# The f16 low part of the middle plane is computed by GpSimd in place of VectorE, for all images but the last

## The chip, the cores and the metric

One core of one Trainium2 chip runs the whole program. The metric is the device time of one execution, in microseconds (us). Engine names are those of the profile: PE is TensorE, PEld its weight loads, DVE is VectorE, ACT is ScalarE, POOL is GpSimd, SP is SyncE, which only issues DMAs here.

## What is computed

Two residual convolution blocks on x of shape 16 x 128 x 32 x 32 (f32), 128 channels in and out, 3x3 kernels:

```python
pooled  = mean(gn(x), axis=(2, 3))
routing = sigmoid(pooled @ w_route.T + b_route)               # 4 experts per image
y       = conv3x3(gn(x), w_experts)                           # mixed over experts by routing
x       = x + silu(batch_norm(y))
x       = x + conv3x3(gn(x), sign(W))
```

`gn` is a group norm with 32 groups of 4 channels, without affine parameters. The second `gn(x)`, times 256, is the middle plane of this text.

## The kernel before, in words

Channels lie on the 128 partitions, the 1024 pixels of an image along the free dimension. All 16 images stay in SBUF in `X`. The loop over t from 1 to 15 works on several images at once, in each of the engines' own programs; what keeps them together are semaphores, and each engine runs its instructions strictly in the order in which they are written.

**First convolution of image t.** ACT and DVE mix the four experts' weights into `U` (DVE `mix`, L781, three instructions of 128x1152 for each image), DVE makes from them the kernels of a Winograd-like transform by rows (`even_rows`, L790 and L791; `kernel_rows`, L801 and L804) and from the normalised image `xn` the transformed rows (`transform_sums`, L813 and L816; `transform`, L824 to L834). PE multiplies at six points, `minus_points` into `pb`, `plus_points` into `pa`, `end_points` into `pe_`, all L402. DVE turns the products back into rows of `y` (`inverse_sums` L841 and L842, which read `pa` in PSUM; `inverse_inner` L847 to L859, SBUF only; `inverse_outer` L867, which reads `pe_` in PSUM). ACT applies the Silu (L608), a DMA from the POOL queue adds `y` to the image in `X` (`residual`, L319; for images 0, 14 and 15 DVE does it, L873 and L881), and ACT takes the variance of the result (`var_mid`, L544), squares the deviations (L551), and PE adds them up over groups (`group_vars`, L376 and L377). DVE scales (`variance`, L745), POOL raises to the power -0.5 (`power`, L315, a tiny instruction of one or two elements per partition), DVE makes the bias (`biases`, L751).

**Second convolution of image t-1.** ACT writes the middle plane twice: `hi` in f16 (L623) and `hn` in f32 (L630). DVE writes `lo = hn - hi` in f16 (`low_part`, L892, 128x1024). PE multiplies the f16 weights `ws`, the signs, first by `hi`, then by `lo` (`sign_half`, L437, 18 matmuls each over two halves, all into `pc`). ACT copies the sum out (`evacuate`, L637), and a DMA from the POOL queue adds it to the output in HBM (`add_output`, L324). `hn` has one buffer: ACT's next `hn` waits for `lo`. `hi` and `lo` have two.

**Order in an image's period on DVE** (t from 2): `mix` x3, `even_rows`, `variance`, half of `kernel_rows`, `biases`, the other half, `inverse_sums`, `inverse_inner`, `inverse_outer`, `low_part(t-1)`, `transform_sums(t+2)`, `transform(t+2)`. **On POOL:** `power(t+2)`, `add_output(t-2)`, `residual(t)`. **On PE:** `minus_points(t)`, `group_vars(t+2)`, `plus_points(t)`, `end_points(t)`, logits, `hi` products of image t-1, `lo` products of image t-1 with `group_means(t+3)` between their halves. At t=1 `low_part(0)` stands between the second and the third `mix`. At t=15 DVE's `low_part(14)` stands ahead of `residual_last`, the bn statistics of image 15 (L731) and the last group norm; the last image's `lo` is made after that.

Of the kernel before, what the change touches and what calls it, by code (L numbers as in the profile page):

```python
# [10 lines left out]
ALU = mybir.AluOpType  # L11
ACT = mybir.ActivationFunctionType

B, C, H, W = 16, 128, 32, 32
# [36 lines left out]
def build(nc, x, w_experts, w_sign, params, out):  # L51
# [6 lines left out]
    with ExitStack() as ctx:  # L58
        def sb(name, shape, dt=F32):
            return ctx.enter_context(nc.sbuf_tensor(name, shape, dt))  # L60
# [4 lines left out]
        def sem(name):  # L65
            return ctx.enter_context(nc.semaphore(name))
# [15 lines left out]
        hn = sb("hn", [C, HW])  # L82
        hi = [sb(f"hi{p}", [C, H, W], F16) for p in range(2)]
        lo = [sb(f"lo{p}", [C, H, W], F16) for p in range(2)]
# [91 lines left out]
        hi_ready = sem("hi_ready")  # L176
        hn_ready = sem("hn_ready")
        lo_ready = sem("lo_ready")
        conv_ready = sem("conv_ready")
# [9 lines left out]
        def img(i):  # L189
            return X[:, i * HW:(i + 1) * HW]  # L190

        def flat(ap):
            return ap.rearrange("p a b -> p (a b)")

        def flat3(ap):
            return ap.rearrange("p t k w -> p (t k w)")
# [19 lines left out]
        def cols(c):  # L216
            return (IN if c < LAG else MID), (2 if c < B else 1)
# [31 lines left out]
        def silus(i):  # L249

            return i + 1 + (i == B - 1)
# [22 lines left out]
        @block.sync  # L274
        def _(sp):
            def load(i):
                sp.dma_start(img(i), x_v[i, :, :]).then_inc(x_loaded[i], 16)

            def load_row(slot, row):
                sp.dma_start(we[:, :, slot, :], we_v[:, row, :, :]).then_inc(we_loaded[slot], 16)  # L280

            sp.dma_start(img(0)[:, 0:BANK], x_halves[0, 0, :, :]).then_inc(x_half_loaded, 16)
            sp.dma_start(img(0)[:, BANK:HW], x_halves[0, 1, :, :]).then_inc(x_loaded[0], 16)
            sp.dma_start(prm[:], params).then_inc(prm_loaded, 16)
            load(1)
            load_row(G1, 1)
            load_row(G0, 0)
            load_row(G2, 2)
            load(2)
            load(3)  # L290
            sp.dma_start(ws_raw[:], ws_v).then_inc(ws_loaded, 16)
            for i in range(4, B):
                sp.wait_ge(x_loaded[i - 3], 16)
                load(i)
            for i in range(B - LATE):
                wait_h(sp, i)
                sp.dma_start(out_v[i, :, :], img(i)).then_inc(h_stored[i], 16)
            done = 0
            for i in range(B - LATE, B):
                for first, last in out_parts(i):  # L300
                    done += 1
                    sp.wait_ge(out_ready, done)
                    sp.dma_start(out_v[i, :, first:last], img(i)[:, first:last]).then_inc(stored, 16)
            sp.wait_ge(stored, 16 * done)
            for p in range(2):
                sp.wait_ge(out_added[p], 16 * (B - LATE) // 2)

        @block.gpsimd
        def _(pool):
            g = nc.gpsimd  # L310

            def power(c):
                a, b = cols(c)
                pool.wait_ge(ve_ready, c + 1)
                g.tensor_tensor(rstd[:, c, a:b], ve[:, c, a:b], nhalf[:, a:b], ALU.pow).then_inc(rstd_ready, 1)  # L315

            def residual(i):
                pool.wait_ge(silu_ready, silus(i))
                g.dma_start(img(i), flat3(y[i % 2][:]), accum_op=ALU.add).then_inc(added[i % 2], 16)  # L319

            def add_output(i):
                pool.wait_ge(h_stored[i], 16)
                pool.wait_ge(evacuated, i + 1)
                g.dma_start(out_v[i, :, :], ev[i % 2][:], accum_op=ALU.add).then_inc(out_added[i % 2], 16)  # L324

            g.memset(nhalf[:], -0.5).then_inc(zeroed, 1)
            g.memset(ones[:], 1.0).then_inc(zeroed, 1)
            g.iota(gdist[:], [[GSIZE, C // GSIZE], [0, GSIZE]], base=0, channel_multiplier=-1) \
             .then_inc(gdist_ready, 1)
            for p in range(2):  # L330
                g.memset(xn[p][:, 0:PH:PH - 1, :], 0.0).then_inc(zeroed, 1)
            pool.wait_ge(zeroed, 1)
            pool.wait_ge(bn_ve_ready, 1)
            g.tensor_tensor(bn_rs[:], bn_ve[:], nhalf[:, 0:1], ALU.pow).then_inc(bn_rs_ready, 1)
            for c in range(LAG):
                power(c)
            for t in range(ND):
                if t not in DVE_RESIDUAL:
                    residual(t)
            for t in range(1, B + 1):  # L340
                power(t + LAG - 1)
                if 0 <= t - 2 < B - LATE:
                    add_output(t - 2)
                if ND <= t < B and t not in DVE_RESIDUAL:
                    residual(t)

# [349 lines left out]
        def _(dve):  # L696
# [45 lines left out]
            def variance(c):  # L742
                a, b = cols(c)
                dve.wait_ge(gvar_ready, c + 1)
                v.tensor_scalar(ve[:, c, a:b], gvar(c, a, b), 1.0 / ACT_SCALE ** 2, GN_EPS / ACT_SCALE ** 2,  # L745
                                ALU.mult, ALU.add).then_inc(ve_ready, 1)
# [11 lines left out]
            def pool_routes(c):  # L758
                if c < B:
                    dve.wait_ge(zr_ready, c + 1)  # L760
                    v.scalar_tensor_tensor(out=pooled[:, c, :], in0=wroute[:], scalar=zr[:, c:c + 1], in1=bshare[:],
                                           op0=ALU.mult, op1=ALU.add).then_inc(pooled_ready, 1)
# [74 lines left out]
            def inverse_sums(t):  # L837
                r = rank(t)
                dve.wait_ge(minus_ready, r + 1)
                dve.wait_ge(m_ready, 3 * r + 2)  # L840
                v.tensor_tensor(flat3(sums[:]), flat3(pa[:]), minus[:], ALU.add).then_inc(sums_ready, 1)  # L841
                v.tensor_tensor(flat3(diffs[:]), flat3(pa[:]), minus[:], ALU.subtract).then_inc(sums_ready, 1)  # L842
# [41 lines left out]
                    half_stats(i, half)  # L884
                aggregate(i, CHAINS - 1, MID, nm_mid_ready, var_mid_ready)

            def low_part(i):
                dve.wait_ge(hn_ready, i + 1)
                dve.wait_ge(hi_ready, i + 1 + (i == B - 1))
                if i >= 2:  # L890
                    dve.wait_ge(conv_ready, 2 * (i - 1))
                v.tensor_tensor(flat(lo[i % 2][:]), hn[:], flat(hi[i % 2][:]), ALU.subtract).then_inc(lo_ready, 1)  # L892

            def output_part(i, n):
# [43 lines left out]
            for t in range(1, B):  # L938

                c = t + LAG - 1  # L940
                if t == 1:
                    variance(c)
                    inverse_sums(t)
                    biases(c)
                    pool_routes(c)
                    inverse_inner(t)
                    inverse_outer(t)
                    mix(t + 1, 2)
                    low_part(t - 1)
                    mix(t + 1, 3)  # L950
                    even_rows(t + 1)
                    kernel_rows(t + 1, -1)
                    kernel_rows(t + 1, 1)
                else:
                    mix(t + 1, 1)
                    mix(t + 1, 2)
                    mix(t + 1, 3)
                    even_rows(t + 1)
                    variance(c)
                    kernel_rows(t + 1, -1)  # L960
                    biases(c)
                    pool_routes(c)
                    kernel_rows(t + 1, 1)
                    inverse_sums(t)
                    inverse_inner(t)
                    inverse_outer(t)
                    low_part(t - 1)
                transform_sums(t + 2)
                if t in DVE_RESIDUAL and ND <= t < B - 1:
                    residual(t)  # L970
                transform(t + 2)
                if t == B - 1:
                    residual_last()
                    variance(CHAINS - 1)
                    biases(CHAINS - 1)
                    output_part(B - 2, 0)
                    output_part(B - 2, 1)
                    low_part(B - 1)
                    for n in range(len(out_parts(B - 1))):
                        output_part(B - 1, n)  # L980

# [23 lines left out]
```

## Time and profile before

| | |
|---|---|
| median of 3 runs | 292.47 us (292.43 to 293.48) |
| the profiled execution, device time | 292.85 us |
| its span, first to last instruction | 291.0 us |
| around the span | 1.85 us |
| PE busy | 276.5 us |
| DVE busy | 255.8 us |
| ACT busy | 185.6 us |
| POOL busy | 41.8 us |
| granted TensorE clock, mean over the span | 0.988 of full speed |

A busy time is the union of the times of an engine's instructions; waits are not in it. The start of a row is counted from the start of the span. In the timeline, a bracket at the end of a row is the idle time ahead of it and what ended that. Two DVE instructions in a row overlap by some 0.08 us in the records, so the cost of one in a full queue is the distance from its start to the next one's start.

### The profile page before, as it was taken

The page shows a single profiled execution, that of the slowest core. Times are in us where ns is not written, and L with a number is a line of the kernel's source. Part 1 is how long each engine was busy: PE and PEld are TensorE (multiplying, and loading weights), DVE is VectorE, ACT ScalarE, POOL GpSimd, SP SyncE. Part 2 cuts the span into 40 slices and gives each one's busy share as a digit, 9 for nine tenths or more (in the row PEclk, how much of TensorE's full clock was granted, in tenths as well). Part 3 has the DMA queues.
Part 4 walks back from the last instruction along what each step waited for, and adds up shares of the span by engine and source line. Part 5 has one row for each costly group of instructions (what it writes and reads, how often), then busy time and mean ns, then how long its engine had stood idle before and what let it go on. Part 6 is the DMA issues. An engine that isn't in the chain of part 4 may idle for free.

```text
span 291.0 us, 3911 instructions
## 1 busy us (share of the span) xinstructions
PE 276.5 (95%) x1342; PEld 190.6 (66%) x1342; DVE 255.8 (88%) x492; ACT 185.6 (64%) x297; POOL 41.8 (14%) x56
## 2 busy tenths in 40 slices
PE   7699789968999999999999999999999999999896
PEld 6544574934849586766758595857677685948454
DVE  4794989999999999999999999999999999941832
ACT  2563668458776858676787778586867774645230
POOL 2102001021212121020212121211202121202000
PEclk9689999999999999999999999999999999999999
DMA  7998813144453525545454435254454544411312
GB/s 220 396 362 288 295 75 72 72 73 104 88 98 87 111 93 83 136 72 146 72 125 73 94 90 115 86 94 123 74 144 73 143 63 86 108 39 9 63 72 74
DMA packets 10963, 34.14 MB, mean 117 GB/s; under 512 B 1216, under 2 KB 3008, under 8 KB 10944
## 3 DMA queue, kind: packets, MB, share of 16 engines
q0 software_dynamic: 3888, 14.16, 28.8%
q1 hardware_dynamic: 7056, 19.74, 18.2%
q8 instruction: 11, 0.18, 0.2%
q14 instruction: 8, 0.07, 0.1%
HBM read 11.34 MB, written 15.73 MB: 93 GB/s over the span
## 4 chain that ended last, share of the span: by engine, by line
PE 78%; DVE 9%; issue 6%; ACT 3%; DMA 2%; POOL 1%; SPq 0%; ACTq 0%; DVEq 0%; POOLq 0%
PE pc L437 36%; PE pa L402 12%; PE pb L402 11%; PE pe_ L402 10%; PE pd L392 4%; DMA X<-x 2%; PE ps L377 1%; POOL rstd L315 1%; ACT y L608 1%; DVE halves L731 1%; PE ps L367 1%; DVE sums L841 1%; PE ps L376 1%; PE pd L353 1%; PE pb L437 1%
## 5 line engine op out<-in xcount | busy, mean ns | idle before, releaser
L437 PE MATMUL pc<-lo,ws 128*128 128x496 f16 (+5 forms) x288 | 64.8, 372 | 0.4 <-DVE lo L892 0.4
L781 DVE SCALAR_TENSOR_TENSOR U<-we,route,U 128x1152 f32<-128x1152 f32 x45 | 63.6, 1414 | 0.9
L437 PE MATMUL pc<-hi,ws 128*128 128x496 f16 (+5 forms) x288 | 62.6, 372 | 0.7 <-ACT hi L623 0.5
L437 PEld LDWEIGHTS pc<-hi,ws 128*128 128x128 f16 x288 | 28.0, 101 | 30.3 <-ACT hi L623 1.1
L437 PEld LDWEIGHTS pc<-lo,ws 128*128 128x128 f16 x288 | 28.1, 102 | 28.8 <-DVE lo L892 1.1
L402 PE MATMUL pa<-V,UM 128*128 128x256 f32 (+1 forms) x180 | 41.8, 382 | 0.0
L402 PE MATMUL pb<-V,UM 128*128 128x256 f32 (+1 forms) x180 | 40.6, 375 | 0.1
L402 PE MATMUL pe_<-V,U 128*128 128x256 f32 (+1 forms) x180 | 40.6, 375 | 0.0
L315 POOL TENSOR_TENSOR rstd<-ve,nhalf 128x2 f32<-128x2 f32 (+1 forms) x19 | 16.8, 886 | 159.7 <-DVE ve L745 159.7
L402 PEld LDWEIGHTS pb<-V,UM 128*128 128x128 f32 x180 | 34.2, 190 | 5.7 <-issue 0.8
L402 PEld LDWEIGHTS pe_<-V,U 128*128 128x128 f32 x180 | 34.2, 190 | 3.8
L402 PEld LDWEIGHTS pa<-V,UM 128*128 128x128 f32 x180 | 33.1, 191 | 3.2
L623 ACT ACTIVATE hi<-X,nbias,rstd 128x1024 f16<-128x1024 f32 (+2 forms) x17 | 20.1, 1190 | 22.8 <-DVE nbias L751 22.8
L544 ACT ACTIVATE junk_mid<-X,nm 128x1024 f32<-128x1024 f32 x15 | 17.2, 1149 | 17.7 <-DMA X<-y 16.3
L563 ACT ACTIVATE xn<-X,nbias,rstd 128x1024 f32<-128x1024 f32 (+2 forms) x17 | 20.0, 1178 | 6.4 <-PE pd L392 6.1
L608 ACT ACTIVATE y<-y,bn_shift,bn_tiles 128x1024 f32<-128x1024 f32 x14 | 17.4, 1240 | 10.4 <-DVE y L867 10.4
L319 POOL DMA_DIRECT2D X<-y x13 | 11.5, 883 | 72.1 <-ACT y L608 72.1
L597 ACT ACTIVATE minus<-pb 128x512 f32<-128x512 f32 x15 | 8.9, 595 | 19.0 <-PE pb L402 19.0
L892 DVE TENSOR_TENSOR lo<-hn,hi 128x1024 f16<-128x1024 f32 x16 | 19.4, 1212 | 1.1 <-ACT hn L630 1.1
L630 ACT ACTIVATE hn<-X,nbias,rstd 128x1024 f32<-128x1024 f32 x16 | 19.6, 1227 | 0.0
L581 ACT ACTIVATE U<-we,route 128x1152 f32<-128x1152 f32 x15 | 18.6, 1240 | 0.0
L813 DVE SCALAR_TENSOR_TENSOR e_rows<-xn 128x1024 f32<-128x1024 f32 x15 | 18.2, 1216 | 0.0
(98 smaller groups left out, 367.9 us busy)
## 6 DMA issues: line engine op xcount, KB each, us to landing
X<-x SPq DMA_DIRECT2D x15, 512.0 KB, 5.2
out<-X SPq DMA_DIRECT2D x14, 512.0 KB, 2.6
out<-ev POOLq DMA_DIRECT2D x14, 512.0 KB, 5.5
X<-y POOLq DMA_DIRECT2D x13, 512.0 KB, 4.5
we<-w_experts SPq DMA_DIRECT2D x3, 768.0 KB, 8.6
out<-X SPq DMA_DIRECT2D x3, 256.0 KB, 2.0
ws_raw<-w_sign SPq DMA_DIRECT2D x1, 576.0 KB, 11.8
X<-x SPq DMA_DIRECT2D x2, 256.0 KB, 2.8
```

The source lines that it names most:

```text
L315: g.tensor_tensor(rstd[:, c, a:b], ve[:, c, a:b], nhalf[:, a:b], ALU.pow).then_inc(rstd_ready, 1)
L402: mm = mm_(bank[:, :, j, c0:c1], weights[:, kx * C:(kx + 1) * C], V[t % 2][:, :, k, c0 + kx - 1:c1 + kx - 1], start=(n == 0), stop=(n == K ...
L437: mm = mm_(rows[:, r0 - first // W:r1 - first // W, c0:c1], ws[:, tap * C:(tap + 1) * C], (hi, lo)[part][i % 2][:, r0 + ky - 1:r1 + ky - 1 ...
L544: activation(junk["mid"][:], img(i), ACT.Square, bias=nm[:, c, MID:MID + 1], scale=1.0 / ROOT_HW, accum_out=var[:, c, MID:MID + 1]).then_i ...
L563: activation(xn[i % 2][:, 1 + first:1 + last, :], img(i).rearrange("p (h w) -> p h w", h=H)[:, first:last, :], ACT.Identity, bias=nbias[:, ...
L581: activation(flat(U[i % 2][:]), flat(we[:, 0, :, :]), ACT.Copy, scale=route[:, i, 0:1]).then_inc(mix_first, 1)
L608: activation(flat3(y[i % 2][:]), flat3(y[i % 2][:]), ACT.Silu, bias=bn_shift[:, 0:1], scale=bn_tiles[:, 0:1], accum_out=ysum[:, i:i + 1]). ...
L623: activation(hi[i % 2][:, first:last, :], img(i).rearrange("p (h w) -> p h w", h=H)[:, first:last, :], ACT.Identity, bias=nbias[:, c, MID: ...
L630: activation(hn[:], img(i), ACT.Identity, bias=nbias[:, c, MID:MID + 1], scale=rstd[:, c, MID:MID + 1]).then_inc(hn_ready, 1)
L781: v.scalar_tensor_tensor(out=flat(U[i % 2][:]), in0=flat(we[:, e, :, :]), scalar=route[:, i, e:e + 1], in1=flat(U[i % 2][:]), op0=ALU.mult ...
L813: v.scalar_tensor_tensor(out=flat3(e_rows[:]), in0=flat(xn[i % 2][:, 0:H, :]), scalar=-4.0, in1=flat(xn[i % 2][:, 2:2 + H, :]), op0=ALU.mu ...
L892: v.tensor_tensor(flat(lo[i % 2][:]), hn[:], flat(hi[i % 2][:]), ALU.subtract).then_inc(lo_ready, 1)
```

## The change

`low_part` leaves the DVE program and enters the POOL program, with the same operands, waits and semaphore; it stands there behind `add_output(t-2)` and ahead of `residual(t)`, for t from 1 to 15 (images 0 to 14). The last image's stays on DVE under the name `low_part_last`.

```diff
@@ gpsimd
+            def low_part(i):
+                pool.wait_ge(hn_ready, i + 1)
+                pool.wait_ge(hi_ready, i + 1)
+                if i >= 2:
+                    pool.wait_ge(conv_ready, 2 * (i - 1))
+                g.tensor_tensor(flat(lo[i % 2][:]), hn[:], flat(hi[i % 2][:]), ALU.subtract).then_inc(lo_ready, 1)
@@ gpsimd, loop over t
                 power(t + LAG - 1)
                 if 0 <= t - 2 < B - LATE:
                     add_output(t - 2)
+                if t < B:
+                    low_part(t - 1)
                 if ND <= t < B and t not in DVE_RESIDUAL:
                     residual(t)
@@ vector
-            def low_part(i):
+            def low_part_last():
+                i = B - 1
                 dve.wait_ge(hn_ready, i + 1)
-                dve.wait_ge(hi_ready, i + 1 + (i == B - 1))
-                if i >= 2:
-                    dve.wait_ge(conv_ready, 2 * (i - 1))
+                dve.wait_ge(hi_ready, i + 2)
+                dve.wait_ge(conv_ready, 2 * (i - 1))
                 v.tensor_tensor(flat(lo[i % 2][:]), hn[:], flat(hi[i % 2][:]), ALU.subtract).then_inc(lo_ready, 1)
@@ vector, loop over t
                     mix(t + 1, 2)
-                    low_part(t - 1)
                     mix(t + 1, 3)
...
                     inverse_outer(t)
-                    low_part(t - 1)
                 transform_sums(t + 2)
...
-                    low_part(B - 1)
+                    low_part_last()
```

## Rows read from the trace of the kernel before

**Rows 1.** Page, part 1: busy time, share of the span, instructions.
```profile
PE 276.5 (95%) x1342; PEld 190.6 (66%) x1342; DVE 255.8 (88%) x492; ACT 185.6 (64%) x297; POOL 41.8 (14%) x56
```

**Rows 2.** Windows: length, busy PE, PEld, DVE, ACT, POOL, PEclk, DMA share, GB/s.
```profile
135.20:151.10 15.90, 15.90 (x82) 11.23 (x81) 15.62 (x30) 11.88 (x20) 2.67 (x3) 1.00 0.47 100
```

**Rows 3.** Chain that ended last, two starts of minus_points: start us, us, what.
```profile
87.37 2.54 PE pb L402 x12
...
246.87 2.54 PE pb L402 x12
```

**Rows 4.** Timeline of POOL, four rstd instructions: start us, us, what.
```profile
26.08 1.65 POOL L315 TENSOR_TENSOR rstd<-ve,nhalf 128x1 f32<-128x1 f32 x1 [15.09 <-DVE ve L745]
...
91.37 0.95 POOL L315 TENSOR_TENSOR rstd<-ve,nhalf 128x2 f32<-128x2 f32 x1 [7.73 <-DVE ve L745]
...
250.70 0.81 POOL L315 TENSOR_TENSOR rstd<-ve,nhalf 128x1 f32<-128x1 f32 x1 [7.73 <-DVE ve L745]
...
278.68 0.56 POOL L315 TENSOR_TENSOR rstd<-ve,nhalf 128x1 f32<-128x1 f32 x1 [10.46 <-DVE ve L745]
```

**Rows 5.** Page, part 5: the group that the change moves.
```profile
L892 DVE TENSOR_TENSOR lo<-hn,hi 128x1024 f16<-128x1024 f32 x16 | 19.4, 1212 | 1.1 <-ACT hn L630 1.1
```

**Rows 6.** Timeline of all engines in one mid-run image, 136 to 147 us.
```profile
136.28 0.39 ACT L551 ACTIVATE dev<-ps,nm 128x1 f32<-128x1 f32 x2
...
137.59 0.28 PE L376 MATMUL ps<-var,gmat 128*128 128x2 f32 x2
...
141.50 1.22 ACT L630 ACTIVATE hn<-X,nbias,rstd 128x1024 f32<-128x1024 f32 x1
...
142.75 0.41 DVE L847 SCALAR_TENSOR_TENSOR outer<-sums 128x256 f32<-128x256 f32 x1
...
144.09 0.75 DVE L867 SCALAR_TENSOR_TENSOR y<-pe_,outer 128x256 f32<-128x256 f32 x2
144.75 1.21 DVE L892 TENSOR_TENSOR lo<-hn,hi 128x1024 f16<-128x1024 f32 x1
...
145.89 1.22 DVE L813 SCALAR_TENSOR_TENSOR e_rows<-xn 128x1024 f32<-128x1024 f32 x1
...
146.50 0.87 POOL L319 DMA_DIRECT2D X<-y  x1 [5.54 <-ACT y L608]
...
146.86 1.77 PEld L437 LDWEIGHTS pc<-lo,ws 128*128 128x128 f16 x9
```

**Rows 7.** Timeline of DVE, the instruction in progress when POOL began an rstd.
```profile
25.92 1.41 DVE L781 SCALAR_TENSOR_TENSOR U<-we,route,U 128x1152 f32<-128x1152 f32 x1
...
250.54 0.55 DVE L801 TENSOR_TENSOR UM<-even,U 128x384 f32<-128x384 f32 x1
```

**Rows 8.** Line 804 by itself: duration ns min/median/max.
```profile
L804 DVE SCALAR_TENSOR_TENSOR UM<-U,even x30: 548/550/552, 31.1 to 252.1; 128x384 f32<-128x384 f32 x30
```

**Rows 9.** Lines 327 and 331 by themselves: duration ns min/median/max.
```profile
L327 POOL MEMSET ones<- x1: 204/204/204, 0.8 to 0.8; 128x128 f32 x1
...
L331 POOL MEMSET xn<- x2: 146/146/146, 1.3 to 1.4; 128x64 f32 x2
```

**Rows 10.** Timeline of the first two sign convolutions: ACT, DVE, PE.
```profile
42.44 1.23 ACT L630 ACTIVATE hn<-X,nbias,rstd 128x1024 f32<-128x1024 f32 x1
...
43.57 1.41 DVE L781 SCALAR_TENSOR_TENSOR U<-we,route,U 128x1152 f32<-128x1152 f32 x1
...
61.09 0.39 PE L381 MATMUL ps<-pooled,ones 128*128 128x4 f32 x2 [1.84 <-DVE pooled L761]
```

**Rows 11.** Timeline of the tail, 267 to 275 us.
```profile
267.78 1.23 ACT L630 ACTIVATE hn<-X,nbias,rstd 128x1024 f32<-128x1024 f32 x1
...
269.51 0.41 DVE L847 SCALAR_TENSOR_TENSOR outer<-sums 128x256 f32<-128x256 f32 x1
...
271.37 1.52 ACT L614 ACTIVATE y<-y,bn_shift,bn_tiles 128x512 f32<-128x512 f32 x2 [2.35 <-DVE y L867]
...
272.78 1.28 DVE L881 TENSOR_TENSOR X<-y,X 128x512 f32<-128x512 f32 x2
```

## The prediction

> **What bounds the kernel now.** I read the busy line first [rows 1]: PE works 276.5 of 291.0 us, DVE 255.8, ACT 185.6, POOL 41.8. That makes PE the bound and POOL the idle engine, but it is an average. The windows show mid-run by itself [rows 2]: in 15.90 us PE is busy for all 15.90 and DVE for 15.62. So there are two engines at the limit, not one. Their paces confirm it: ten images apart, `minus_points` starts on PE at 87.37 and 246.87, so 15.95 us an image [rows 3]; the rstd instruction, which follows DVE's `variance` at once, starts on POOL at 91.37 and 250.70, so 15.93 an image [rows 4]. DVE sets its own pace and is 0.02 us an image ahead. Taking work off DVE gains nothing there; adding more than 0.02 us an image to it is paid as soon as PE's small reserves are used up.
>
> **What the change removes.** Fifteen of the sixteen `lo` instructions of DVE, 1.21 us each [rows 5]. In the full queue each costs the distance to the next start, 144.75 to 145.89, so 1.14 us [rows 6]. What that is worth alone:
> - Mid-run: nothing, PE covers it by 0.02 us an image.
> - Start: PE waits 1.84 us for DVE's `pooled` at 61.09 [rows 10], at the end of a DVE stretch that holds `lo(0)`. The 1.14 us come off here.
> - Tail: `lo(14)` stands ahead of the residual of image 15. That residual starts at 272.78 and ends at 274.06, but its second half also waits for the second Silu, done at 271.37 + 1.52 = 272.89 [rows 11]. With 0.05 us for the semaphore and 0.68 for the half it would end at 273.62: 0.44 us gained, not 1.14.
> Together -1.58 us. This is the whole possible gain.
>
> **What it adds.** Fifteen POOL instructions that read 2 x 1024 elements a partition and write 1024. No row shows such an instruction. Two things have to be priced: its length, and what it does to DVE.
>
> Length: two memsets of 128 and 64 elements take 204 and 146 ns [rows 9], so 0.91 ns for an element written. At the same rate the two reads take 2048 x 0.91 = 1.86 us. Behind the instruction that it waited for, an rstd needed another 0.4 us (below), so about 2.3 us in all. `hn` ends at 142.72 and PE loads the first weights of the `lo` products at 146.86 [rows 6]; 4.1 us are free. On POOL's queue the new instruction waits for `hn`; behind it stands only the DMA of `residual(t)`, which now starts at 146.50 after 5.54 us of idling, so an instruction done by 145.5 holds up nothing on its own queue. The power of the next image comes later still. ACT's next `hn`, which waits for `lo`, is a period away.
>
> What it does to DVE: the four rstd rows tell [rows 4, 7]. With DVE quiet, one element takes 0.56 us (278.68). At 26.08 it takes 1.65: DVE's `mix`, two SBUF inputs, was running until 25.92 + 1.41 = 27.33, and POOL ended 0.40 behind that. At 250.70 it takes 0.81: L801, also with two SBUF inputs, ran until 251.09, and POOL ended 0.42 behind that, while the next DVE instruction was already queued. So the two engines do exclude each other: POOL waits out the instruction in progress and then gets its turn ahead of the next. For two elements the turn is too short to show on DVE (all thirty L804, some of them just behind such a turn, last 548 to 552 ns [rows 8]). For 2048 it should show in full.
>
> So I take it that DVE is shut out while POOL reads: 1.86 us. From below this is bounded by 1.2 us, what DVE itself needs for the instruction [rows 5]; from above by the whole length behind DVE's last instruction, 1.86 + 0.4, rounded up to 2.4. I choose 1.9, the value of the reads alone, since L804 was not held until the end of the rstd beside it. In mid-run POOL asks at about 142.8, when L847 has just started (142.75, ends 143.16 [rows 6]); the next instruction would have begun 0.08 before that end, so DVE's block is 1.9 + 0.08 = 1.98 us. L867, which reads PSUM, and needs no turn, does not help: it is queued behind.
>
> The Trainium skill ("SBUF — State Buffer", Who interferes with whom) says that a DVE instruction with two SBUF inputs contends with a GpSimd instruction that reads SBUF, and that the loser is shut out for the whole instruction. The trace agrees with the first half; L804's unchanged 550 ns speaks against the second for a short instruction. By the second half the block would be the upper bound, 2.4 us. The skill ("GPSIMD Engine Reference", Performance versus the Vector engine) gives 4497 ns for 2048 f32 elements of a two-input operation, from which I estimate 2.25 us here; no row of this trace has such an instruction.
>
> **The sum.**
> - Per image: 1.98 - 1.14 - 0.02 = 0.82 us more on DVE. For t = 1 the place is another (`hn` ends at 43.67, inside a `mix` that runs until 44.98 [rows 10]), the block the same. It counts for t = 1 to 12: 12 x 0.82 = 9.84.
> - The block stands ahead of `y`, the removed instruction stood behind it. So `y`, its Silu, the residual's DMA and `var_mid` come 1.98 us later in their own period. PE's `group_vars` had 137.59 - 136.67 = 0.92 us of reserve behind the deviations [rows 6]. Cost, once, as PE falls behind DVE: 1.98 - 0.92 = 1.06.
> - t = 14 has no transforms for later images, so DVE has room, and PE only keeps what it has lost.
> - Tail: `hn(14)` ends at 269.01, DVE is in L842, which reads PSUM, so POOL starts at 269.1 and L847 goes from 269.51 to 271.0, +1.5. The second Silu is then done at 274.4, the residual of image 15 at 275.1 in place of 274.06 [rows 11]: +1.05.
> Sum 11.95 us on the profiled execution's 292.85: 304.8. That execution stands 0.38 above the median of 292.47, so 304.4 as a median. With the bounds 1.2 and 2.4 the same terms give 12 x 0.12 + 0.36 + 0.35 = 2.1 and 12 x 1.32 + 1.56 + 1.55 = 18.9: 294.6 to 311.4 as medians.
>
> **The rivals.** About 0.5%, 1.5 us, is what a measurement can tell from no change.
> - *DVE is not held up* (the reads are buffered, or DVE's second operand goes first and POOL fits in). Then the gain above is all: 292.47 - 1.58 = 290.9, just past the bound on the faster side. For: 550 ns of L804. Against: POOL's own waits, which end exactly with DVE's instructions. Chance 0.13.
> - *The two share the port, not by turns*, so that DVE loses about the time of one operand, 0.93 us. Per image that is 0.93 - 1.14, a gain that PE swallows; start -0.21, tail +0.5: 292.8, no change. For: nothing here excludes it. Against: as above. Chance 0.12.
> - *POOL is the late one*: it is served in pieces, each behind a DVE instruction. DVE loses little, but past 4.1 us after `hn` each us of `lo` comes on PE's path in 14 images. At 5.0 us: 14 x 0.9 = 12.6, less the tail's 0.44: 304.6. For: 1.1 us lost behind one `mix`. Against: it was served ahead of L804. Chance 0.10, and far above the range if POOL were served only when DVE pauses, since DVE hardly does.
> - The step itself is certain to be moved; with 0.03 for what I don't see, 0.62 is left for the forecast.
>
> **How the numbers follow.** The forecast lies on the slower side over its whole range; with the third rival and 0.03 that gives slower 0.75. The first rival lies on the edge, 0.11 faster and 0.02 same; the second is 0.11 same and 0.01 faster: faster 0.12, same 0.13. The forecast's own range is 294.6 to 311.4; the range of 8 in 10 reaches down over the first two rivals, 290.8, and up to 311.5.
>
> **What would show each step.** `lo` on POOL with a mean near 2.3 us and, mid-run, begun just behind `hn`. L847 or the instruction behind it (L850) lasting some 1.9 us longer than 0.41, or a gap ahead of it, and e_rows starting just behind L867. A pace of 16.8 us between `minus_points` starts, with PE idle mostly ahead of `group_vars` or `hi`. DVE's busy time up though it has fifteen instructions fewer. I am wrong if L847 to L859 keep their 0.41 us and 0.34 us spacing, if the pace stays at 15.95, or if PE waits for `lo`.

## The result and the profile after

The changed kernel takes 309.77 us (309.53 to 312.48, 4 runs), the kernel before, run beside it, 292.98 us (292.43 to 294.95). The ratio is 1.058, 95% interval 1.050 to 1.066: slower by 17 us. The forecast was 304.4 us in a range of 290.8 to 311.5. The span went from 291.0 to 307.7 us, by 16.7; the working below uses the spans.

Page of the changed kernel: the busy line, and the groups that belong to the steps of the prediction (line engine op, tiles, forms and count | busy us, mean ns | idle before, releaser). Lines after 326 have moved by 9: L847 is now L856, L892 is the POOL line L331, and so on.

```profile
PE 282.8 (92%) x1342; PEld 190.7 (62%) x1342; DVE 269.8 (88%) x477; ACT 186.8 (61%) x297; POOL 75.8 (25%) x71
...
L331 POOL TENSOR_TENSOR lo<-hn,hi 128x1024 f16<-128x1024 f32 x15 | 33.4, 2226 | 21.1 <-ACT hn L639 21.1
...
L856 DVE SCALAR_TENSOR_TENSOR outer<-sums 128x256 f32<-128x256 f32 x15 | 29.4, 1959 | 0.0
...
L376 PE MATMUL ps<-nm,gmat 128*128 128x2 f32 (+1 forms) x34 | 6.2, 252 | 13.9 <-ACT junk_mean L533 9.5
```

POOL has taken 34 us more [rows 1], as it should: 15 x 2.2. But DVE, with fifteen instructions of 1.21 us fewer, is busy 14 us longer. The group that shows most of it is L856, `outer<-sums`, a 128x256 instruction that took 0.41 us [rows 6] and now has a mean of 1.96. The last row is the other piece of news: PE now waits 13.9 us ahead of L376 (3.9 before), and 9.5 of them (1.0 before) are `group_means` waiting for ACT's `junk_mean`, that is for `mean_in`, the ACT instruction that sums up a later input image.

Timeline of the changed kernel in one mid-run image:

```profile
148.91 1.23 ACT L639 ACTIVATE hn<-X,nbias,rstd 128x1024 f32<-128x1024 f32 x1
...
150.23 2.12 POOL L331 TENSOR_TENSOR lo<-hn,hi 128x1024 f16<-128x1024 f32 x1 [1.25 <-ACT hn L639]
150.26 2.38 DVE L856 SCALAR_TENSOR_TENSOR outer<-sums 128x256 f32<-128x256 f32 x1
...
152.56 0.41 DVE L859 SCALAR_TENSOR_TENSOR outer<-diffs 128x256 f32<-128x256 f32 x1
...
153.56 0.74 DVE L876 SCALAR_TENSOR_TENSOR y<-pe_,outer 128x256 f32<-128x256 f32 x2
154.23 1.21 DVE L822 SCALAR_TENSOR_TENSOR e_rows<-xn 128x1024 f32<-128x1024 f32 x1
154.34 1.24 ACT L617 ACTIVATE y<-y,bn_shift,bn_tiles 128x1024 f32<-128x1024 f32 x1 [2.29 <-DVE y L876]
155.06 1.77 PEld L446 LDWEIGHTS pc<-lo,ws 128*128 128x128 f16 x9
...
158.23 0.38 PE L376 MATMUL ps<-nm,gmat 128*128 128x2 f32 x2 [0.90 <-ACT junk_mean L533]
```

POOL takes up `lo` 0.09 us behind `hn`'s end, 0.03 us before DVE begins L856. L856 lasts 2.38 us, and the next DVE instruction begins 2.30 us behind it where 0.33 is normal: a block of 1.97 us. L859, L876 and e_rows behind it have their old durations. `lo` takes 2.12 us and is done 2.7 us before PE loads the first weights for it, at 155.06. The Silu, which used to start at 144.87 in an image whose rstd started at 139.17, so 5.70 us behind it, starts 7.75 us behind it now (154.34 less 146.59): 2.05 us later.

The same image in the windows, as [rows 2] (length, busy PE, PEld, DVE, ACT, POOL, PEclk, DMA share, GB/s), and the chain that ended last for the same image (start us, us, what):

```profile
143.42:160.54 17.12, 16.22 (x82) 11.18 (x81) 16.65 (x29) 12.02 (x20) 4.86 (x4) 1.00 0.44 93
```

```profile
146.59 0.96 POOL rstd L315
148.11 0.47 DVE UM L810
148.58 0.42 DVE UM L813
149.05 0.69 DVE sums L850
149.74 0.60 DVE diffs L851
150.34 1.20 DVE outer L856
151.54 1.01 issue
153.64 0.68 DVE y L876 x2
154.34 1.34 ACT y L617 x2
156.02 1.03 issue
157.05 1.14 ACT junk_mean L533 x2
158.62 1.93 PE pc L446 x9
160.54 2.54 PE pb L411 x12
163.71 0.96 POOL rstd L315
```

Before, this chain was PE alone for almost two hundred microseconds. Now it goes round through POOL, DVE, ACT and PE in 17.12 us: from rstd over DVE's kernel rows, `sums`, `diffs`, the stretched L856 (with 1.01 us of it put down as "issue"), `y`, the Silu on ACT, then `mean_mid`, the first mix and `mean_in` on ACT, `group_means` on PE, nine `lo` products, `minus_points`, `group_vars`, and back to the next rstd.

**Where the 16.7 us are.** From the starts of `minus_points` (pb) in both traces:

| stretch | before | after | more by |
|---|---|---|---|
| up to image 2's | 51.03 | 51.87 | 0.84 |
| image 2's to 3's | 20.22 | 22.89 | 2.67 |
| image 3's to 13's, ten intervals | 159.50 | 171.25 | 11.75, 1.17 each |
| image 13's to 15's | 31.77 | 32.12 | 0.35 |
| image 15's to the last output instruction | 25.90 | 27.04 | 1.14 |

The first 0.84 us aren't the change's: the rstd at 26.08 before [rows 4] is at 26.92 after, ahead of any changed instruction, and in the ten traces of this case it lies anywhere from 25.19 to 27.57. From image 1's `minus_points` to image 2's nothing is lost, 19.72 us in both.

### The profile page after: what moved, and what is told of

Read it like the earlier page. It is cut to its first block, busy times and chain, and to the rows that moved or that the text cites. A ratio compares the mean times of both kernels' runs of the same rounds, so it can differ in the third digit from the quotient of the medians.

```text
span 307.7 us, 3911 instructions
## 1 busy us (share of the span) xinstructions
PE 282.8 (92%) x1342; PEld 190.7 (62%) x1342; DVE 269.8 (88%) x477; ACT 186.8 (61%) x297; POOL 75.8 (25%) x71
## 4 chain that ended last, share of the span: by engine, by line
PE 40%; DVE 28%; issue 13%; ACT 11%; POOL 6%; DMA 1%; SPq 0%; ACTq 0%; DVEq 0%; POOLq 0%
PE pc L446 15%; PE pb L411 11%; ACT y L617 5%; DVE outer L856 4%; POOL rstd L315 4%; ACT junk_mean L533 4%; PE pd L401 4%; DVE sums L850 3%; PE pa L411 3%; DVE y L876 3%; DVE diffs L851 3%; DVE outer L859 2%; DVE UM L810 2%; DVE UM L813 2%; PE pe_ L411 2%
## 5 line engine op out<-in xcount | busy, mean ns | idle before, releaser
L790 DVE SCALAR_TENSOR_TENSOR U<-we,route,U 128x1152 f32<-128x1152 f32 x45 | 65.3, 1452 | 1.0
L446 PE MATMUL pc<-hi,ws 128*128 128x496 f16 (+5 forms) x288 | 65.4, 383 | 0.5 <-ACT hi L632 0.3
L446 PEld LDWEIGHTS pc<-hi,ws 128*128 128x128 f16 x288 | 28.7, 103 | 32.1 <-issue 3.7
L331 POOL TENSOR_TENSOR lo<-hn,hi 128x1024 f16<-128x1024 f32 x15 | 33.4, 2226 | 21.1 <-ACT hn L639 21.1
L856 DVE SCALAR_TENSOR_TENSOR outer<-sums 128x256 f32<-128x256 f32 x15 | 29.4, 1959 | 0.0
L376 PE MATMUL ps<-nm,gmat 128*128 128x2 f32 (+1 forms) x34 | 6.2, 252 | 13.9 <-ACT junk_mean L533 9.5
```

What stands on the lines that cost most here:

```text
L331: g.tensor_tensor(flat(lo[i % 2][:]), hn[:], flat(hi[i % 2][:]), ALU.subtract).then_inc(lo_ready, 1)
L446: mm = mm_(rows[:, r0 - first // W:r1 - first // W, c0:c1], ws[:, tap * C:(tap + 1) * C], (hi, lo)[part][i % 2][:, r0 + ky - 1:r1 + ky - 1 ...
L790: v.scalar_tensor_tensor(out=flat(U[i % 2][:]), in0=flat(we[:, e, :, :]), scalar=route[:, i, e:e + 1], in1=flat(U[i % 2][:]), op0=ALU.mult ...
L856: v.scalar_tensor_tensor(out=outer[:, :, 0, :], in0=sums[:, :, 1, :], scalar=-0.25, in1=sums[:, :, 0, :], op0=ALU.mult, op1=ALU.add).then_ ...
```

## The experiments

Each was timed in three rounds beside the kernel before. "Pace" is the distance from one image to the next in mid-run, between the starts of the rstd instruction on POOL or of `minus_points` on PE. The lines shown are of two neighbouring images; the table at the end has means over ten.

**The removal alone.** The question is what DVE's lost work is worth when nothing is put on POOL.

```diff
+            for p in range(2):
+                g.memset(flat(lo[p][:]), 0.0).then_inc(lo_zeroed, 1)
...
+                n = HW if i == B - 1 else 2
+                dve.wait_ge(lo_zeroed, 2)
-                v.tensor_tensor(flat(lo[i % 2][:]), hn[:], flat(hi[i % 2][:]), ALU.subtract).then_inc(lo_ready, 1)
+                v.tensor_tensor(flat(lo[i % 2][:])[:, 0:n], hn[:, 0:n], flat(hi[i % 2][:])[:, 0:n],
+                                ALU.subtract).then_inc(lo_ready, 1)
```

> The kernel before with DVE's lo cut to 2 of 1024 columns for images 0 to 14 (lo is cleared once at the start; the output lacks the low part there). It is the removal alone, without anything on POOL. My theory, that mid-run PE covers DVE's 1.14 us an image and only the start and the tail give something: 290.9 to 292, pace of minus_points still 15.95 us. Rival, that DVE's full queue costs something in every image: 15.95 falls, total below 288.

Measured: 292.13 us, ratio 0.9954 (0.9923 to 0.9985). In its trace the pace is 15.95. From `minus_points` of image 2 to that of image 3 it is 19.22 us in place of 20.22, a gain of 1.00; from that of image 15 to the end 0.43 less (span 290.2 less 262.31, against 291.0 less 262.68). Together 1.43 us. The median lies 0.13 us above the forecast's range, beside a kernel before that ran at 293.53 in these rounds. So the removal is worth nothing in mid-run, and its whole worth is about half a percent.

**POOL busy, but writing only.**

```diff
-                g.tensor_tensor(flat(lo[i % 2][:]), hn[:], flat(hi[i % 2][:]), ALU.subtract).then_inc(lo_ready, 1)
+                g.memset(flat(lo_junk[:]), 0.0)
+                g.memset(flat(lo[i % 2][:]), 0.0).then_inc(lo_ready, 1)
```

> The changed kernel with POOL's subtraction replaced by two memsets of 128x1024 f16 (one into a spare tile, one into lo), with the same waits and at the same place; the output lacks the low part for images 0 to 14. POOL is busy at the same moment but reads nothing. If only POOL's reading shuts DVE out, L856 takes its 0.41 us again and the time is that of e1_removed within 0.7 us. Rival A, any POOL instruction blocks DVE: L856 stretched to the length of the memsets. Rival B, the change is slow because PE waits for POOL's late lo: still near 309.

Measured: 291.93 us, ratio 0.9935 (0.9912 to 0.9957). Groups of this kernel (L858 is `outer<-sums`):

```profile
L332 POOL MEMSET lo_junk<- 128x1024 f16 x15 | 14.2, 947 | 20.2 <-ACT hn L641 20.2
L333 POOL MEMSET lo<- 128x1024 f16 x15 | 14.2, 947 | 0.0
...
L858 DVE SCALAR_TENSOR_TENSOR outer<-sums 128x256 f32<-128x256 f32 x15 | 6.2, 416 | 0.0
```

POOL is busy for 2 x 0.95 us at the same place in the program, behind the same waits, and L858 has its old 0.42. The time is that of the removal alone. So neither POOL's being busy, nor its place in the queue, nor the moment at which `lo` is ready costs anything. What is left is that the instruction reads.

**One input in place of two.**

```diff
-                g.tensor_tensor(flat(lo[i % 2][:]), hn[:], flat(hi[i % 2][:]), ALU.subtract).then_inc(lo_ready, 1)
+                g.tensor_copy(flat(lo[i % 2][:]), hn[:]).then_inc(lo_ready, 1)
```

> The changed kernel with POOL's subtraction replaced by a copy of hn into lo (f32 to f16), one input in place of two; the output is not the sum of a high and a low part. If the block is the time of the reads, 1024 in place of 2048 elements give POOL about 1.1 us and DVE a block of about 1.0, less than the 1.14 us removed: pace 15.95, 291 to 293. Rival, the block is a fixed cost of POOL's loop and not of its reads: POOL stays at 2.1 us, L856 near 2.4, time near 309.

Measured: 294.99 us, ratio 1.0048 (1.0023 to 1.0073), 2 us above the first theory's range and far from the second's. In its trace the kernel loses 2.8 us from the `minus_points` of image 1 to that of image 15: 1.10 from image 2 to 3 (21.32 us for 20.22), 1.14 from image 3 to 4 (17.09 for 15.95), and some 0.06 in each of nine intervals more. Of the first two, 1.7 us are not DVE's. Behind a wait of 2.08 us for `junk_mean` PE ran slower, with a granted clock of 0.50, the 1.2 GHz level, from 72 to 74 us, and these two groups took 2.71 and 3.78 us in place of 2.07 and 2.70:

```profile
69.33 2.71 PE L446 MATMUL pc<-lo,ws 128*128 128x512 f16 x9
71.83 3.78 PE L411 MATMUL pb<-V,UM 128*128 128x256 f32 x12
```

In mid-run the clock was whole. Timeline of this kernel there:

```profile
143.91 1.03 POOL L331 CAST lo<-hn 128x1024 f16<-128x1024 f32 x1 [1.22 <-ACT hn L639]
143.96 1.26 DVE L856 SCALAR_TENSOR_TENSOR outer<-sums 128x256 f32<-128x256 f32 x1
...
145.14 0.41 DVE L859 SCALAR_TENSOR_TENSOR outer<-diffs 128x256 f32<-128x256 f32 x1
```

Half the elements read, half the length, 1.03 us, and L856 lasts 1.26: a block of 0.85 us, where the subtraction's was 1.97. The block goes with the reads, or with the length of an instruction that reads; the two were halved together here. But the pace is 16.01 and not 15.95, although DVE has less to do than before (0.85 for 1.14 us). Something else than DVE's queue or PE's work sets it: the pace fell by 17.12 - 16.01 = 1.11 us, L856 from 2.38 to 1.26, by 1.12. That is a loop in which L856 stands once.

**Is it that loop?** ACT's `mean_in`, on which `group_means` waits, is moved from behind the Silu to ahead of it.

```diff
+                if t >= 2 and t + LAG < B:
+                    mean_in(t + LAG)
                 silu(t)
...
                 if t + LAG < B:
-                    mean_in(t + LAG)
+                    if t < 2:
+                        mean_in(t + LAG)
                     var_in(t + LAG)
```

> The changed kernel with ACT's mean_in(t+3) moved from behind silu, mean_mid and mix to ahead of silu (for t from 2), into ACT's idle time there; nothing left out. In the changed kernel DVE alone needs 15.93 - 1.14 + 1.97 = 16.76 us an image, the pace is 17.12. If the other 0.36 is a loop over the late silu, ACT's mean_in and PE's group_means, the pace falls to 16.8 and the time by 10 x 0.35 to about 306. Rival, DVE's queue alone sets the pace: no change, 309.8.

Measured: 306.49 us, ratio 1.0434 (1.0380 to 1.0488). Pace 16.74, the mean of ten intervals between rstd starts, as forecast from DVE's queue (16.76). PE no longer waits for `mean_in`, and what is left is DVE's queue. Here POOL came 0.06 us behind L859, this kernel's `outer<-sums`, in place of 0.03 ahead of it, and had to wait its turn:

```profile
165.80 0.41 DVE L859 SCALAR_TENSOR_TENSOR outer<-sums 128x256 f32<-128x256 f32 x1
165.86 2.35 POOL L331 TENSOR_TENSOR lo<-hn,hi 128x1024 f16<-128x1024 f32 x1 [1.85 <-ACT hn L639]
166.14 2.36 DVE L862 SCALAR_TENSOR_TENSOR outer<-diffs 128x256 f32<-128x256 f32 x1
...
168.42 0.41 DVE L869 SCALAR_TENSOR_TENSOR y<-diffs 128x256 f32<-128x256 f32 x1
```

The instruction in progress keeps its 0.41 us, POOL's takes 2.35 with the wait, and the next DVE instruction, L862, takes 2.36. From L862's start to the next, L869's, it is 2.28 us where 0.33 is normal, a block of 1.95. Whoever comes first, DVE pays the same.

**The same subtraction later.** POOL starts when DVE comes to the two instructions that read PSUM.

```diff
                 pool.wait_ge(hi_ready, i + 1)
+                pool.wait_ge(y_ready, 4 * i + 2)
```

> The changed kernel with one more wait: POOL's subtraction starts only when DVE has finished the third and fourth row group of y (L868), so that it begins under the two L876, which read PSUM. Nothing is left out. If what counts is only which DVE instructions stand in POOL's way, the first 0.6 us of the 2.1 are free and y is no longer late: DVE loses 1.55 in place of 1.97, net 0.41 us an image, pace 16.3 to 16.4, total about 297. Rival, a later lo makes PE wait and the time rises above 309; another, L876 is held up as well: pace as before the edit, 17.1.

Measured: 299.56 us, ratio 1.0211 (1.0185 to 1.0238).

```profile
141.59 0.95 POOL L315 TENSOR_TENSOR rstd<-ve,nhalf 128x2 f32<-128x2 f32 x1 [8.24 <-DVE ve L755]
...
146.51 0.75 DVE L877 SCALAR_TENSOR_TENSOR y<-pe_,outer 128x256 f32<-128x256 f32 x2
146.83 2.12 POOL L332 TENSOR_TENSOR lo<-hn,hi 128x1024 f16<-128x1024 f32 x1 [3.45 <-DVE y L869]
147.17 2.87 DVE L823 SCALAR_TENSOR_TENSOR e_rows<-xn 128x1024 f32<-128x1024 f32 x1
...
158.05 0.95 POOL L315 TENSOR_TENSOR rstd<-ve,nhalf 128x2 f32<-128x2 f32 x1 [8.24 <-DVE ve L755]
```

L877, `y` from `pe_` in PSUM, keeps its 0.75 us for two, though POOL begins in the middle of it. The block falls on e_rows: 2.87 us in place of 1.21, so 1.66, and 1.66 - 1.14 = 0.52 us net an image. Pace 16.46 (141.59 to 158.05), which is 15.93 + 0.52 and a rounding. The 0.52 was forecast at 0.41, as POOL started 0.24 us behind the signal and not 0.1. PE does not wait for the later `lo`. Two things are gained against the change: 0.31 us of the block, which fell from 1.97 to 1.66, and the loop, as the block no longer stands ahead of `y`. The total is 2.6 us above the forecast, of which the 0.11 us an image make 1.3; the rest was not traced. Of the change's 17 us more than half are gone with one wait added.

**The tail alone.** Only `lo(14)` on POOL, beside the bn statistics.

```diff
+                if t == B - 1:
+                    i = t - 1
+                    pool.wait_ge(hn_ready, i + 1)
+                    pool.wait_ge(hi_ready, i + 1)
+                    pool.wait_ge(conv_ready, 2 * (i - 1))
+                    pool.wait_ge(h_ready, h_before(B - 1) + 2)
+                    g.tensor_tensor(flat(lo[i % 2][:]), hn[:], flat(hi[i % 2][:]), ALU.subtract).then_inc(lo_ready, 1)
...
                     inverse_outer(t)
-                    low_part(t - 1)
+                    if t < B - 1:
+                        low_part(t - 1)
```

> The kernel before, with only lo(14) on POOL, started when DVE has made the residual of image 15, so that it runs beside the bn statistics, which read one SBUF input. If only DVE's two-input instructions contend, the two bn_stats keep 0.68 us each and POOL its 2.12; the residual ends 0.43 us earlier, PE gets lo(14) about 0.35 us later than now: 292.0 to 293, no change that can be measured. Rival, any DVE instruction that reads SBUF is held up: bn_stats stretched by 2 us, total 294 or more.

Measured: 293.03 us beside 293.33 of before, ratio 0.9992 (0.9974 to 1.0010).

```profile
274.52 1.28 DVE L738 BATCH_NORM_STATS2 halves<-X 128x6 f32<-128x512 f32 x2
274.79 2.12 POOL L352 TENSOR_TENSOR lo<-hn,hi 128x1024 f16<-128x1024 f32 x1 [5.58 <-DVE X L888]
...
276.96 2.08 PE L444 MATMUL pc<-lo,ws 128*128 128x512 f16 x9 [0.29 <-POOL lo L352]
```

Two bn_stats take 1.28 us together, as before, although POOL's subtraction begins in the first of them and lasts beyond the second. With one SBUF input DVE was not held up. PE waits 0.29 us for `lo`, which takes back most of the 0.43 us that the removal gives at the residual. No version of the move gained anything measurable: this was the best of them.

**Half on each engine.** POOL makes columns 0 to 511, started as in the later version; DVE makes the rest at its old place; PE and ACT wait for both.

```diff
+                pool.wait_ge(y_ready, 4 * i + 2)
-                g.tensor_tensor(flat(lo[i % 2][:]), hn[:], flat(hi[i % 2][:]), ALU.subtract).then_inc(lo_ready, 1)
+                g.tensor_tensor(flat(lo[i % 2][:])[:, 0:BANK], hn[:, 0:BANK], flat(hi[i % 2][:])[:, 0:BANK],
+                                ALU.subtract).then_inc(lo_ready, 1)
...
+                v.tensor_tensor(flat(lo[i % 2][:])[:, BANK:HW], hn[:, BANK:HW], flat(hi[i % 2][:])[:, BANK:HW],
+                                ALU.subtract).then_inc(lo_ready, 1)
```

> POOL makes columns 0 to 511 of lo, started as in e5_later, and DVE columns 512 to 1023 at the place where the kernel before made all of them. Nothing is left out. POOL's half takes 1.1 us, of which 0.6 lie under the two L876; DVE waits the other 0.5 and spends 0.6 on its own half: 1.1, what it spent before. Pace 15.95, total 292.5 to 294. Rival, an instruction on POOL costs DVE a fixed time: pace above 16.3, total above 296.

Measured: 294.94 us, ratio 1.0067 (1.0045 to 1.0089). POOL's half takes 1.15 us, DVE's half starts at 145.94 and e_rows at 147.22, so 1.28 us, where all of `lo` cost 1.14. Pace 16.09. The forecast of 15.95 had set that cost at 1.1; the total is 0.9 us above its range.

**The addition without the removal.** DVE's `lo` stays, POOL does it once more into a spare tile.

```diff
+            def read_again(i):
+                pool.wait_ge(hn_ready, i + 1)
+                pool.wait_ge(hi_ready, i + 1)
+                g.tensor_tensor(flat(lo_junk[:]), hn[:], flat(hi[i % 2][:]), ALU.subtract).then_inc(read_done, 1)
...
+                if t < B:
+                    read_again(t - 1)
...
+                wait(act, read_done, i)
```

> The kernel before, DVE's lo kept, and POOL does the subtraction once more into a spare tile at the place and time of the changed kernel; ACT's next hn waits for it too. It is the added part of the change without the removed part. DVE then needs 15.93 + 1.97 = 17.9 us an image, more than the loop of 17.12: pace 17.9, total 318 to 320. Rival, POOL only lengthens the loop over y, silu and group_means by its block and DVE's queue has room: pace 17.1, about 310.

Measured: 322.77 us, ratio 1.1012 (1.0992 to 1.1032).

```profile
133.56 0.95 POOL L317 TENSOR_TENSOR rstd<-ve,nhalf 128x2 f32<-128x2 f32 x1 [7.72 <-DVE ve L755]
...
151.43 0.95 POOL L317 TENSOR_TENSOR rstd<-ve,nhalf 128x2 f32<-128x2 f32 x1 [7.73 <-DVE ve L755]
...
155.07 2.35 POOL L326 TENSOR_TENSOR lo_junk<-hn,hi 128x1024 f16<-128x1024 f32 x1 [1.84 <-ACT hn L640]
```

Pace 17.88. Here too POOL came just behind an `outer<-sums`, and the block on the instruction after it was 1.94 us, so DVE's queue needs 15.93 + 1.94 = 17.87. The forecast total was 3 us too low, the pace right.

**All paces together.** d is the block ahead of `y`. DVE's queue is 15.93, less 1.14 where `lo` is off it, plus the block wherever it stands. The loop is 15.15 plus d, where 15.15 is the change's pace less its block, 17.12 - 1.97. PE needs 15.95.

| kernel | d | DVE's queue | loop | measured pace |
|---|---|---|---|---|
| before | 0 | 15.93 | 15.15 | 15.95 |
| removal alone | 0 | 14.9 | 15.15 | 15.95 |
| one input | 0.85 | 15.64 | 16.00 | 16.01 |
| the change | 1.97 | 16.76 | 17.12 | 17.12 |
| mean_in first | 1.95 | 16.74 | shorter | 16.74 |
| later | 0 | 16.45 | 15.15 | 16.46 |
| half on each | 0 | 16.07 | 15.15 | 16.09 |
| both | 1.94 | 17.87 | 17.09 | 17.88 |

In every row the pace is the largest of the three, to 0.02 us. The rows of before and of the change fix the three constants, 15.93, 15.95 and 15.15; the other six rows are tests. Of these one, the one input, tests the loop where it is the longest, and `mean_in` first tests it by taking it away; in the others DVE's queue or PE decides. (For the removal alone the queue has 0.07 us in it for the two columns that DVE still made; it decides nothing.)

## Why the prediction was right, point by point

- **Two engines at the limit.** Right. The removal alone gave 1.43 us where the sum said 1.58: start 1.00 for 1.14, tail 0.43 for 0.44, mid-run nothing.
- **POOL's length.** Forecast 2.3 us with the wait for its turn; measured 2.12 when it came first, 2.35 behind a short DVE instruction, 3.21 behind a `mix` (image 1). The rate read off two memsets was a little low: 1.86 us for the reads, where the instruction takes 2.12 without a wait.
- **DVE shut out while POOL reads.** Right, and this is what the case turns on. Forecast 1.98 us a time, measured 1.97. That it fits to 0.01 us is luck, as 1.9 was a choice between bounds of 1.2 and 2.4. The write-only run excludes POOL's being busy and its place, and the doubled run shows the block with nothing removed.
- **That L876 doesn't help, being queued behind.** Right, and the later start shows the reverse: once POOL's instruction lies partly under it, the block is 1.66 us and no longer 1.97.
- **"Cost, once, as PE falls behind DVE: 1.98 - 0.92".** This step failed. The late `y` was followed along one path, the residual's DMA, `var_mid` and `group_vars`, and its cost booked once. The late Silu also delays ACT's `mean_in`, which stands behind it on ACT's queue, and PE's `group_means` waits for that, and from there the path closes on the next `y`. A lateness in a closed loop is paid in every image. The pace was 17.12 and not 16.77: 1.17 us an image where the sum had 0.82. The ten intervals from image 3 to 13 cost 11.75 us and not 8.2. The sign that the prediction named, PE idle ahead of `group_vars` or `hi`, did not come: PE idled ahead of `group_means`. The path could have been found beforehand, since the kernel before takes it once, in image 2, where its chain that ended last reads:

```profile
59.51 0.96 POOL rstd L315
...
67.92 1.14 ACT junk_mean L524 x2
69.11 0.39 PE ps L367 x2
```

- **Images 1 and 2.** The sum had 0.82 each. Image 1's block costs nothing up to image 2's `minus_points`, since PE waits for DVE only behind that; it is paid in the next interval, which took 2.67 us more. All of them are DVE's. In the chain of that interval the rstd starts 9.22 us behind image 2's `minus_points` (61.09 less 51.87), where it was 8.48 (59.51 less 51.03): 0.74 later, image 1's block less the instruction taken away. And `group_means` starts 11.53 us behind that rstd (72.62 less 61.09), where it was 9.60 (69.11 less 59.51): 1.93 later, which is image 2's block ahead of `y`, passed on whole by the Silu and `mean_in`. So the stretch took 2.67 us where the sum had 2 x 0.82 + 1.06 = 2.70; that they agree is luck, as the 1.06 was worked out for the path over `group_vars`, where PE did not wait longer than before (1.2 us in all, 1.1 before). The kernel with `mean_in` first, where this path is cut, lost only 0.53 us in the same interval (20.75 for 20.22). The chain's row in the changed kernel:

```profile
61.09 0.96 POOL rstd L315
```

- **Tail.** Forecast +1.05, measured +1.14; the Silu halves and the residual came late as said.
- **The rivals.** "DVE is not held up" and "the two share the port" fall with 1.97 us at L856. "POOL is the late one" falls, since `lo` was 2.7 us early.

So the sign and what POOL does to DVE were right, and what the late `y` does further on was wrong. The total was short by the loop: 3.5 us in the ten intervals and 0.4 in the last two, with 0.1 in the tail. The 0.84 us ahead of image 2 are no part of it. That 309.77 still lies below the upper bound is in part luck: the 311.4 stood for a block of 2.4 us, the block was 1.97, and a path that the sum did not have filled the room.

One thing between image 2 and image 3 looks like a cost and is none. In the changed kernel PE ran at the lower clock level for a while, and 18 `hi` products took 6.73 us in place of 3.97. Timeline of PE (brackets are its waits), then one window, with PEclk at 0.50, the 1.2 GHz level:

```profile
62.67 0.59 PE L390 MATMUL ps<-pooled,ones 128*128 128x4 f32 x2 [2.58 <-DVE pooled L770]
63.56 6.73 PE L446 MATMUL pc<-hi,ws 128*128 128x512 f16 x18 [0.30 <-ACT hi L632]
...
72.62 0.38 PE L376 MATMUL ps<-nm,gmat 128*128 128x2 f32 x2 [0.42 <-ACT junk_mean L533]
```

```profile
64.00:66.00 2.00, 2.00 (x6) 0.71 (x5) 2.00 (x4) 1.97 (x4) 1.27 (x1) 0.50 0.88 162
```

Slow as they were, PE came to `group_means` 0.42 us before ACT's `junk_mean` was done, so the 2.76 us fell into time that PE would have waited. In the one-input kernel the same drop came behind `junk_mean`, with nothing to wait for, and was paid. The length of PE's wait alone does not decide whether the level falls: with `mean_in` first it did not behind 2.59 us (the 18 products took 3.98), and in the tail kernel it did behind 1.85 (5.39 us), where the kernel before has 1.84 and kept its clock. What does was not tried.

## What to carry to other kernels

Before moving an elementwise operation from DVE to POOL, look at what DVE runs beside it: here a POOL instruction that reads SBUF stopped DVE's two-input SBUF instructions for about its own length, so 1.14 us taken off cost 1.97 us. If it has to be on POOL, start it under DVE work that reads PSUM or has one SBUF input. And where an instruction comes late, follow every consumer until the path ends or returns to itself: once round is a one-time cost only if the path does not close.

## What the runs showed that had not been expected

- The block is a little shorter than POOL's instruction: 1.97 of 2.12 us for two inputs, 0.85 of 1.03 for one. The Trainium skill ("SBUF — State Buffer", SBUF: two separate sides) says that the loser is shut out for the whole instruction. These runs agree to within 0.2 us, so the doubt that the prediction took from L804's 550 ns was worth little: at the 1 ns an element measured here, two elements are too few to show a block.
- The same page of the Trainium skill ("SBUF — State Buffer", Who interferes with whom) says that only POOL instructions that read contend with DVE's two-input ones, and that a DVE instruction with one SBUF input, outside its two-port modes, does not. The memsets (L858 at 0.42 us) and the bn statistics (1.28 us for two) agree.
- POOL's cost a column on 128 partitions is near 1 ns for a copy (1.03 us for 1024), 0.93 ns for a memset to f16, and 2.07 ns for the subtraction.
- Order did not matter between the two engines: 0.03 us ahead of L856 or 0.06 us behind it, DVE lost 1.97 us in the one case and 1.95 in the other.
